# Cross-attention scores in three PSUM banks of four, six and six heads instead of four banks of four

## What is computed

```python
x = x + scan_layer(layernorm(x))
q = split_heads(layernorm(x) @ Wq) * DH ** -0.5          # 16 heads of 64
k, v = null key/value + the context's 64 keys/values      # J = 65 per head
attn = softmax(q @ k.T)                                   # 1024 x 65 per head and batch
x = x + layernorm_affine((attn @ v).reshape(n, 1024) @ Wout)
g, u = bitlinear(layernorm(x), w_gate), bitlinear(layernorm(x), w_up)   # 1024 wide
x = x + bitlinear(silu(g) * u, w_down)
```

## Time and profile before

| | us |
|---|---|
| median of 3 runs (531.52 to 532.60) | 531.68 |
| the profiled execution: device time | 531.91 |
| its span (first to last instruction) | 530.1 |
| TensorE busy (matmul) | 477.0 |
| VectorE busy | 427.8 |
| ScalarE busy | 325.1 |
| GpSimd busy | 304.8 |

### The profile page before, as it was taken

How to read it: one execution, slowest core, us unless ns; L and a number is a source line. 1 busy time by engine, 2 the same in 40 slices (tenths; PEclk the granted TensorE clock), 3 DMA queues, 4 the chain that set the end, 5 groups by cost and what they waited for, 6 DMA issues and landing times.

```text
span 530.1 us, 9241 instructions
## 1 busy us (share of the span) xinstructions
PE 477.0 (90%) x2926; PEld 389.5 (73%) x2954; DVE 427.8 (81%) x936; ACT 325.1 (61%) x450; POOL 304.8 (57%) x482
## 2 busy tenths in 40 slices
PE   1899999989988998999999999999999999998562
PEld 0676787767767887978887888888888878867221
DVE  4899998968527667889889889989898899886763
ACT  4433333236333434788878888888888788876450
POOL 2211233810001467788787787787877877888731
PEclk9989999999999999999999999999999999999995
DMA  8995000240000000011122122212221211122342
GB/s 263 324 350 215 1 0 1 40 80 1 1 1 1 1 1 6 6 31 36 37 54 49 39 47 45 51 36 53 44 46 36 55 41 46 38 53 51 70 100 69
DMA packets 68173, 32.06 MB, mean 60 GB/s; under 512 B 50720, under 2 KB 66336, under 8 KB 68128
## 3 DMA queue, kind: packets, MB, share of 16 engines
q1 hardware_dynamic: 68128, 31.50, 23.2%
HBM read 15.24 MB, written 4.19 MB: 37 GB/s over the span
## 4 chain that ended last, share of the span: by engine, by line
PE 54%; DVE 30%; issue 6%; POOL 4%; DMA 4%; ACT 1%; DVEq 1%; POOLq 0%
PE psum L1128 22%; PE psum L1370 10%; PE psum L1375 10%; DVE region_d L987 5%; DVE mx L984 4%; DVE amax L1016 3%; PE psum L1144 3%; DVE region_a L870 3%; DMA region_d<-region_d 2%; PE psum L1231 2%; PE psum L1248 1%; DVE st L1081 1%; DVE xs L812 1%; PE psum L1261 1%; DMA region_c<-region_d 1%
## 5 line engine op out<-in xcount | busy, mean ns | idle before, releaser
L523 POOL TENSOR_TENSOR region_d<-region_d,rden 128x1024 f32<-128x1024 f32 x32 | 60.9, 1903 | 90.5 <-DVE rden L1001 90.5
L1128 PE MATMUL psum<-Mhi,xT2hi 128*128 128x260 f32 x256 | 75.0, 293 | 0.2
L1128 PE MATMUL psum<-Mlo,xT2hi 128*128 128x260 f32 x256 | 72.4, 283 | 0.0
L1128 PE MATMUL psum<-Mhi,xT2lo 128*128 128x260 f32 x256 | 72.3, 283 | 0.0
L1370 PE MATMUL psum<-VW,region_d 128*128 128x256 f32 x256 | 61.1, 381 | 4.8 <-DVE pTn L1045 4.8
L1375 PE MATMUL psum<-VW,region_d 128*128 128x256 f32 x256 | 60.5, 379 | 0.0
L1370 PEld LDWEIGHTS psum<-VW,region_d 128*128 128x128 f32 x256 | 48.1, 190 | 14.9 <-DVE pTn L1045 6.4
L1375 PEld LDWEIGHTS psum<-VW,region_d 128*128 128x128 f32 x256 | 48.6, 190 | 6.6
L984 DVE TENSOR_REDUCE mx<-psum 128x8 f32<-128x520 f32 x64 | 44.2, 691 | 6.4 <-PE psum L1128 5.2
L1128 PEld LDWEIGHTS psum<-Mhi,xT2hi 128*128 128x128 f32 x256 | 48.2, 188 | 1.3 <-issue 1.0
L1128 PEld LDWEIGHTS psum<-Mlo,xT2hi 128*128 128x128 f32 x256 | 48.3, 189 | 0.0
(11 more groups left out here) (140 smaller groups left out, 1219.5 us busy)
## 6 DMA issues: line engine op xcount, KB each, us to landing
out_dram<-xs SPq DMA_DIRECT2D x32, 128.0 KB, 1.9
xs<-in_x_dram SPq DMA_DIRECT2D x1, 2560.0 KB, 13.5
VW<-in_L_xattn_Wkv_dram SPq DMA_DIRECT2D x1, 2048.0 KB, 12.1
region_b<-in_L_xattn_Wkv_dram SPq DMA_DIRECT2D x1, 2048.0 KB, 17.3
xs<-in_x_dram SPq DMA_DIRECT2D x3, 512.0 KB, 6.8
region_w<-in_L_ffn_w_gate_dram SPq DMA_DIRECT2D x2, 512.0 KB, 9.8
region_w<-in_L_ffn_w_up_dram SPq DMA_DIRECT2D x2, 512.0 KB, 7.8
region_w<-in_L_ffn_w_down_dram SPq DMA_DIRECT2D x8, 128.0 KB, 5.7
```

What stands on the lines that cost most here:

```text
L523: pool.tensor_tensor(p2[:, v, 0:H * MK].rearrange("p (h j) -> p h j", j=MK), e[:, :, 0:MK], rden[:, v, :].unsqueeze(2).broadcast_to([P, H, ...
L1128: mm = pe.matmul(dst, lhsT, rhs, start=i == 0, stop=i == len(terms) - 1)
```

## The change

The scores of a tile go to three banks: heads 0 to 3 to bank 2 (part 0), heads 4 to 9 to bank 0 and 10 to 15 to bank 1 (part 1). Before, part 0 was heads 0 to 7 in banks 0 and 1, part 1 heads 8 to 15 in banks 2 and 3. Gate now goes to banks 2 and 3, up to banks 0 and 1, the other way round than before. The semaphore counts stay. The wait for the copies of the folded values moves from part 1 of tile 0 to part 0.

```diff
--- before.py
+++ after.py
@@ -47,12 +47,12 @@
     NG = T // GT
     HC = INNER // P
     J = MK + 1
-    BANKS_S = 4
-    HB = H // BANKS_S
+    S_BANKS = ((2, 0, 4), (0, 4, 10), (1, 10, 16))
+    S_FIRST = 4
     CC = CTX // P
     FC = FI // P
     BM = B * MK
-    assert (KD, GT, DH, MK, H, N // GN) == (2, 4, 64, 64, 16, 2) and BM == 256 and HB * J <= 512
+    assert (KD, GT, DH, MK, H, N // GN) == (2, 4, 64, 64, 16, 2) and BM == 256 and (H - S_FIRST) * J <= 1024
 
     x_t = x.rearrange("b n d -> (b n) d").rearrange("(t p) d -> p t d", p=P)
     out_t = out.rearrange("b n d -> (b n) d").rearrange("(t p) d -> p t d", p=P)
@@ -110,7 +110,7 @@
         nv = sbuf("nv", [P, 1])
         absum = sbuf("absum", [P, 3])
         wrecip = sbuf("wrecip", [P, 3])
-        mx = sbuf("mx", [P, 2, H // 2])
+        mx = sbuf("mx", [P, H])
         den = sbuf("den", [P, H])
         rden = sbuf("rden", [P, 2, H])
         st3 = sbuf("st3", [P, 6])
@@ -690,7 +690,7 @@
                 act.wait_ge(zw_done, n - 4)
                 if positive(n - 6):
                     act.wait_ge(hq_done, n - 6)
-                act.activation(hid3[v], banks(0, 2).rearrange("p b n -> p (b n)"), ACT.Silu,
+                act.activation(hid3[v], banks(2, 2).rearrange("p b n -> p (b n)"), ACT.Silu,
                                scale=zw[:, (n - 5) % 4, 0:1]).then_inc(silu_ready, 1)
 
             def norm3(n, v):
@@ -976,19 +976,24 @@
 
             def softmax_half(n, hh, u):
 
-                scores = banks(2 * hh, 2)[:, :, 0:HB * J].rearrange("p b (h j) -> p b h j", j=J)
+                rest = (H - S_FIRST) // 2
+                if hh == 0:
+                    scores = bank(2, S_FIRST * J).rearrange("p (h j) -> p h j", j=J)
+                    top = mx[:, 0:S_FIRST]
+                    less = e2[:, u, 0:S_FIRST * J].rearrange("p (h j) -> p h j", j=J)
+                    tops = top.unsqueeze(2).broadcast_to([P, S_FIRST, J])
+                else:
+                    scores = banks(0, 2)[:, :, 0:rest * J].rearrange("p b (h j) -> p b h j", j=J)
+                    top = mx[:, S_FIRST:H].rearrange("p (b h) -> p b h", h=rest)
+                    less = e2[:, u, S_FIRST * J:].rearrange("p (b h j) -> p b h j", b=2, j=J)
+                    tops = top.unsqueeze(3).broadcast_to([P, 2, rest, J])
                 dve.wait_ge(sim_psum, 2 * n + hh + 1)
                 if hh == 0:
                     if positive(2 * n - 2):
                         dve.wait_ge(p_ready, 2 * n - 2)
-                dve.tensor_reduce(mx[:, hh, :].rearrange("p (b h) -> p b h", h=HB), scores, AX.X, ALU.max) \
-                    .then_inc(max_done, 1)
+                dve.tensor_reduce(top, scores, AX.X, ALU.max).then_inc(max_done, 1)
                 dve.wait_ge(max_done, 2 * n + hh + 1)
-                dve.tensor_tensor(
-                    e2[:, u, hh * 2 * HB * J:(hh + 1) * 2 * HB * J].rearrange("p (b h j) -> p b h j", b=2, j=J),
-                    scores,
-                    mx[:, hh, :].rearrange("p (b h) -> p b h", h=HB).unsqueeze(3).broadcast_to([P, 2, HB, J]),
-                    ALU.subtract).then_inc(sim_sub, 1)
+                dve.tensor_tensor(less, scores, tops, ALU.subtract).then_inc(sim_sub, 1)
 
             def exp_sum(n, slot):
 
@@ -1006,7 +1011,7 @@
                 dve.wait_ge(up_psum, n - 4)
                 dve.wait_ge(zw_done, n - 4)
                 dve.wait_ge(silu_ready, n - 4)
-                dve.scalar_tensor_tensor(out=hid3[v], in0=banks(2, 2).rearrange("p b n -> p (b n)"),
+                dve.scalar_tensor_tensor(out=hid3[v], in0=banks(0, 2).rearrange("p b n -> p (b n)"),
                                          scalar=zw[:, (n - 5) % 4, 1:2], in1=hid3[v], op0=ALU.mult, op1=ALU.mult) \
                     .then_inc(h_ready, 1)
 
@@ -1295,17 +1300,17 @@
             def scores_half(n, hh, u4, q, b):
 
                 pe.wait_ge(xT2_lo_ready, q + 1)
-                if n == 0 and hh == 1:
+                if n == 0 and hh == 0:
                     pe.wait_ge(vw_first, HC)
                     pe.wait_ge(vw_second, HC)
                 if positive(2 * n - 1 + hh):
                     pe.wait_ge(sim_sub, 2 * n - 1 + hh)
                 if positive(n - 7):
                     pe.wait_ge((silu_ready, h_ready)[hh], n - 7)
-                for g in (2 * hh, 2 * hh + 1):
-                    mm = group(bank(g, HB * J),
+                for b_, first, last in S_BANKS[hh:1 + 2 * hh]:
+                    mm = group(bank(b_, (last - first) * J),
                                [(xT[:, (u4 // 2) % 2, k, (u4 % 2) * P:(u4 % 2 + 1) * P],
-                                 m[:, k, b, g * HB * J:(g + 1) * HB * J])
+                                 m[:, k, b, first * J:last * J])
                                 for k in range(KD) for xT, m in ((xT2hi, Mhi), (xT2hi, Mlo), (xT2lo, Mhi))])
                 mm.then_inc(sim_psum, 1)
 
@@ -1322,13 +1327,13 @@
                 if positive(n - 5):
                     pe.wait_ge(silu_ready, n - 5)
                 for j in range(2):
-                    mm = group(bank(j), [(nT3[:, slot, k, :], wgT[:, k, j * 512:(j + 1) * 512]) for k in range(KD)])
+                    mm = group(bank(2 + j), [(nT3[:, slot, k, :], wgT[:, k, j * 512:(j + 1) * 512]) for k in range(KD)])
                 mm.then_inc(gate_psum, 1)
                 pe.wait_ge(sim_sub, upto(2 * n + 6, 2 * T))
                 if positive(n - 5):
                     pe.wait_ge(h_ready, n - 5)
                 for j in range(2):
-                    mm = group(bank(2 + j), [(nT3[:, slot, k, :], wuT[:, k, j * 512:(j + 1) * 512]) for k in range(KD)])
+                    mm = group(bank(j), [(nT3[:, slot, k, :], wuT[:, k, j * 512:(j + 1) * 512]) for k in range(KD)])
                 mm.then_inc(up_psum, 1)
 
             def stages2_3(n, u4):
```

## The result

The changed kernel takes 542.52 us (median of 6 runs, 541.18 to 542.93), the one before 532.33 (6 runs): a ratio of 1.0182, 95% interval 1.016 to 1.0204, so 9.7 us slower by the ratio, 10.2 by the medians. The forecast had the sign and 7.4; 539.1 and the range up to 541.6 were too low. Of all executions of the kernels here two ran in a slow state (897.61 with the split alone, 635.09 of the kernel before) and count in no ratio. The profiled execution takes 541.75, its span 540.0, 9.9 more than before.

The account below looks back on a forecast made before the run. TensorE and VectorE hand over to each other, leg P TensorE's, leg D VectorE's. Start 2.45, steps 2 to 4 1.5 and legs P with step 5 3.5 sum to 7.4: 531.68 + 7.4 = 539.1, range 535.2 to 541.6.

Parts of the forecast that it names:

- part 1 seen: When VectorE sees the last scores matmul of part 1 done: forecast 3.10 us after the first scores matmul.
- the 2.02 behind it: VectorE's way from seeing part 1's scores to the start of the up matmuls, forecast at 2.02 us.
- leg D: Stretch between starts of up matmuls without pair transposes, 10.40 us before; read as VectorE's, forecast to cost nothing.
- no wait, by 0.03: In leg D VectorE is ready for part 1 at 329.49, scores seen at 329.46: no wait, cost nothing.
- legs P: Stretches between starts of up matmuls, after even steps, with pair transposes; 10.48 us before, read as TensorE's own work.
- The wide matmul: Scores matmul of 390 columns, forecast at 0.1755 us; a tile's scores 2.82 instead of 2.88.
- rival (1): Leg D waits too, 0.1 in 11 legs, and 390-column matmuls cost 0.180: 540.7; chance 0.12.
- 0.31 later: In legs P VectorE waits 0.41 for part 1, so up starts 0.31 later; 11 x 0.315 = 3.5.
- Steps 2 to 4: First steps without gate or up, VectorE already waiting for scores: 0.5 longer each, 1.5 in all.
- Steps -2 to 1: Start: tile 0's scores wait for VectorE's last copy of folded values; output product of step 1 2.45 later.
- Banks cost nothing: Gate and up changing places costs nothing: gate waits for part 0, freed earlier, up for part 1 as before.
- No slack later: Nothing later has slack for the delay: the chain is closed from step 5 to the end.

Follow-up runs that it names:

- the split alone: Changed kernel with parts of four and twelve heads kept, but banks, gate and up and the wait for the copies as before the change: 540.92, ratio 1.0155.
- the order with the maximum first: Kernel before, with VectorE's maximum of the hidden values moved ahead of the output product's statistics: 530.71, ratio 0.9957.
- The three splits: Heads per part: 4 and 12 (changed kernel, 542.52), 8 and 8 (kernel before, 532.33), 12 and 4 (gate and up as before the change, 546.48).
- the exchange alone: Kernel before, still eight heads per part, with the banks of parts, gate and up exchanged and part 0 waiting for the copies: 534.68, ratio 1.0043.
- taking VectorE's old wait away: Changed kernel, with VectorE's maximum of the hidden values moved ahead of the output product's statistics: 540.67, ratio 1.0158.

## Why the prediction was right or wrong

The path was right; the sizes of its terms were short, and one term was missing. The step that failed is the interval from the first scores matmul to part 1 seen, put at 3.10 and measured at 3.15 to 3.16, with the 2.02 behind it, which is 2.04. By it leg D, "no wait, by 0.03", was put at nothing and cost 0.64 over twelve legs, and the ten legs P cost 3.81 instead of 3.15. The start and steps 2 to 5 were short by 0.5 more. The missing term is TensorE's clock at the end, 0.8 in the profiled execution. Point by point:

- *What bounds the kernel.* Right. Leg P was TensorE's, leg D VectorE's: the latter was shown by the order with the maximum first. The three splits behave as the path "scores seen, then VectorE's instructions, then up" says, in 11.05 forecast and 11.03 measured at the widest.
- *VectorE's prices.* Right: 0.42 and 0.97 measured.
- *The wide matmul.* Wrong by the step that drew a line between 260 columns at 0.120 and 512 of stage 1 at 0.228. It costs 0.179, at the upper bound of one and a half narrow ones (0.180). So a tile's scores take 2.96 from the first of them to the transposes, as before: from 24 matmuls and weight loads to 18 nothing is saved. The rule in the Trainium skill, "TensorE: Matmul & The Clock Gate", section "Back-to-back issue gap", would give 165 ns for isolated matmuls of 390 columns and 111 for 260; these rows, 179 and 120, don't agree with it for either width.
- *Leg D, "no wait, by 0.03".* Wrong as a size: part 1 is seen 3.16 after the first scores matmul, not 3.10, so VectorE waits 0.05 there. This was rival (1), which put 0.1 on it and the wide matmul at 0.180. Its sum, 9.0, is close to the 9.1 that the terms came to; it had a chance of 0.12.
- *Leg P, "0.31 later".* The mechanism as told, the term 0.08 short in the leg shown (0.39): 0.05 of it from the scores matmuls, whose last starts 2.78 after the first and not 2.73, 0.02 from the 2.02 to up, 0.01 from the way to the scores. Over the ten legs that is 0.66, and with the 0.64 of the legs D it makes the 1.3 missing between steps 5 and 29.
- *Steps 2 to 4.* 0.54 each instead of 0.50, by the same interval.
- *Steps -2 to 1.* 2.80 instead of 2.45. The first scores matmul starts 0.25 after the last copy's end (162.21 after 160.67 + 1.29), not 0.07: 0.18 of the 0.35. Another 0.10 lies in the wide matmuls of tile 2: VectorE sees them 2.42 after the first (173.40 to 175.82), before it was 1.71 (172.00 to 173.71), so 0.71 more where 0.61 was forecast.
- *Banks cost nothing.* Right in the steps; shown by the exchange alone.
- *"No slack later".* Right: nothing is given back after step 5. But the sum had no term for TensorE's clock in the last 60 us, which made 0.8 in the profiled execution.
- *The range.* All terms rest on one interval, first scores matmul to part 1 seen, so they were short together. Against the profiled span 9.1 of 9.9 come from the terms, where 7.4 were forecast. The upper end had no room for the 0.8 of the clock on top. Besides, 539.1 was laid on the median of three runs, 531.68; the six runs of the kernel before have 532.33, so 0.65 of the 3.4 between 539.1 and 542.52 is no part of the change.

## What to carry to other kernels

Before splitting work between two engines unevenly, write down for each part when it is seen and what the second engine still has to do after the last one: with a producer and a consumer of nearly equal speed the consumer's share behind the last part is pure latency, and a large last part lengthens it, while a large first part starts the consumer late. A delay at a place where both engines hand over in a ring is paid in every round. When a loop has two limits 0.05 apart, removing one gives next to nothing: after the change, taking VectorE's old wait away (0.34 in leg D of the kernel before) gave 0.01 there.

## What the runs showed of the hardware

- The scores matmuls (float32r in the kernel, f32 in the rows) of 260 and of 390 columns, with a new weight load for each, cost 0.120 and 0.179 us: 0.46 ns per column both, at a granted clock of 1.00. An aligned start gave 0.177. The 0.417 ns per column of 2.4 GHz isn't reached, and fewer, wider matmuls didn't help.
- After an idle of 2.07 us (before: 2.08) in front of step 0 the clock fell in one trace and not in another, with the same instructions on TensorE up to there: from 172 to 174 it was granted at 0.50, that is 1.2 GHz, with the maximum first, and at 1.00 in the kernel before. Scores of tile 2 and the output product behind them, in the order with the maximum first, then in the kernel before:

```profile
172.36 0.42 PE L1128 MATMUL psum<-Mlo,xT2hi 128*128 128x260 f32 x1
...
174.75 2.17 PE L1370 MATMUL psum<-VW,region_d 128*128 128x256 f32 x8
```

```profile
172.20 0.28 PE L1128 MATMUL psum<-Mlo,xT2hi 128*128 128x260 f32 x1
...
173.51 1.89 PE L1370 MATMUL psum<-VW,region_d 128*128 128x256 f32 x8
```

From the second scores matmul to the output product it is 2.39 at the lower clock and 1.31 at the full one. A difference of 1 us between two profiles of such a kernel can be that alone.
